# Attention weights of sum scores: one fp32 product max(row, column) in place of two fp8 masks and split fp16 factors

## What is computed

```
h     = relu(layernorm(x));  Wh = h @ W
s, t  = Wh @ a[:128], Wh @ a[128:]
e     = leaky_relu(s[:, None] + t[None, :], 0.2)      # 1024 x 1024 per graph
alpha = softmax(e where adj != 0)                     # rows
x     = x + alpha @ Wh        # 2nd layer; the 4th adds elu(alpha @ Wh)
```

## Time and profile before

| what | value |
|---|---|
| median of 3 runs | 1722.07 us (1720.83 to 1725.84) |
| the profiled execution's own time | 1729.38 us |
| its span | 1727.6 us |
| granted TensorE clock, mean over the span | 0.952 of full speed |
| busy share of the span: PE, DVE, ACT | 87%, 77%, 69% |

### The profile page before, as it was taken

How to read it: one execution, slowest core, us unless ns; L and a number is a source line. 1 busy time by engine, 2 the same in 40 slices (tenths; PEclk the granted TensorE clock), 3 DMA queues, 4 the chain that set the end, 5 groups by cost and what they waited for, 6 DMA issues and landing times. The chain is left out here.

```text
span 1727.6 us, 33849 instructions
## 1 busy us (share of the span) xinstructions
PE 1495.8 (87%) x12740; PEld 1205.6 (70%) x12740; DVE 1323.3 (77%) x3869; ACT 1190.0 (69%) x1841; POOL 182.4 (11%) x201
## 2 busy tenths in 40 slices
PE   3999996999456799999999999999999999999863
PEld 3999996555243676868768687686876868768652
DVE  3666663788356688989889898898998989987753
ACT  2777773222247778889788887888878888785841
POOL 3443320000000100000000000000000000000000
PEclk9999997999777899999999999999999999999976
DMA  9989972566412012222122221222222222111011
GB/s 191 209 197 207 200 159 76 180 242 246 147 49 74 24 57 69 73 62 60 58 80 74 62 58 60 80 74 62 56 62 80 74 62 56 50 56 50 13 30 33
DMA packets 108456, 162.03 MB, mean 94 GB/s; under 512 B 9344, under 2 KB 59136, under 8 KB 106240
## 3 DMA queue, kind: packets, MB, share of 16 engines
q1 hardware_dynamic: 85248, 117.86, 22.8%
q0 software_dynamic: 18432, 33.56, 10.5%
q10 hardware_dynamic: 4608, 8.39, 1.4%
HBM read 151.40 MB, written 41.94 MB: 112 GB/s over the span
## 5 line engine op out<-in xcount | busy, mean ns | idle before, releaser
L1283 PE MATMUL ps<-fac_A,mask_A 128*128 128x258 f16 x2048 | 243.5, 274 | 30.5 <-DVE agg L927 16.7
L1347 PE MATMUL ps<-hV,wts 128*128 128x129 f32 x2048 | 252.6, 279 | 11.4 <-DVE xC L959 4.9
L1283 PE MATMUL ps<-fac_C,mask_C 128*128 128x258 f16 x2048 | 237.7, 274 | 22.1 <-DVE mask_C L922 15.5
L1347 PEld LDWEIGHTS ps<-hV,wts 128*128 128x128 f32 x2048 | 241.2, 194 | 18.4 <-DVE xC L959 12.9
L1283 PEld LDWEIGHTS ps<-fac_A,mask_A 128*128 128x128 fp8e4 x2048 | 196.3, 98 | 72.5 <-DVE agg L927 28.6
L1283 PEld LDWEIGHTS ps<-fac_C,mask_C 128*128 128x128 fp8e4 x2048 | 196.6, 98 | 58.6 <-issue 10.0
L307 ACT ACTIVATE maskT<-ps 128x1024 fp8e4<-128x1024 bf16 x128 | 131.3, 1025 | 54.2 <-PE ps L341 42.2
L1185 ACT ACTIVATE lk<-ps 128x1024 f32<-128x1024 f32 x128 | 131.3, 1026 | 38.8 <-DVE wts L947 23.8
L947 DVE SCALAR_TENSOR_TENSOR wts<-lk,wts 128x1024 f32<-128x1024 f32 x128 | 154.4, 1218 | 2.3 <-ACT wts L1187 2.2
L1335 PE MATMUL ps<-g_hi,ag_hi 128*128 128x512 f16 x256 | 98.9, 386 | 51.4 <-ACT wts L1187 36.0
L1163 ACT ACTIVATE mask_A<-s_row,steep_t_A 128x1024 fp8e4<-128x1024 f32 x128 | 141.3, 1143 | 1.8
(11 more groups left out here) (240 smaller groups left out, 3226.8 us busy)
## 6 DMA issues: line engine op xcount, KB each, us to landing
adj_b<-in_adj POOLq DMA_DIRECT2D x128, 256.0 KB, 9.1
maskT_scratch<-maskT SPq DMA_DIRECT2D x16, 1024.0 KB, 6.8
ring_A<-maskT_scratch SPq DMA_DIRECT2D x64, 256.0 KB, 3.1
off<-maskT_scratch SPq DMA_DIRECT2D x32, 512.0 KB, 4.4
ring_C<-maskT_scratch SPq DMA_DIRECT2D x64, 256.0 KB, 3.6
xa<-in_x SPq DMA_DIRECT2D x16, 512.0 KB, 4.2
whT_scratch<-whT_s ACTq DMA_DIRECT2D x32, 256.0 KB, 6.5
whT_b<-whT_scratch SPq DMA_DIRECT2D x16, 512.0 KB, 4.7
```

The lines of the kernel that those rows point to most:

```text
L1283: last = nc.tensor.matmul(Q_SLOTS[c % 2][:, k, 0:XW], m_fp8[x][:, k, j, c * P:c * P + P], fac[x][:, k, j, :], start=(j == 0), stop=(j == T ...
L1347: last = nc.tensor.matmul(Q_SLOTS[c // 2 % 2][:, c % 2, 0:PW], wts[:, j, c * P:c * P + P], hV[b % 2][:, j, :], start=(j == 0), stop=(j == ...
```

## The change

The weights of A and C are made as an fp32 tile: adjacency byte x max(row_e, least), where `row_e` = exp(0.8 (t + top)) runs along the row and `least` = exp(-0.8 (s - top)) is one value per partition; the remaining factor exp(s - top) goes with the node values (`hP`). Both attentions then use the `weigh` of B (64 fp32 products of 129 columns).

- Gone: `indicate`, `make_below`, `make_above`, `high`, `low`, `up`, `gather`, `quotients`, `attend`, the second set of factors, and the tiles mask_A, mask_C, fac, prod, up_part, agg, s_row, lk.
- New on VectorE: `weights` (one 128 x 1024 product per tile, 16 per round), `shares` (reciprocals of two output tiles' row sums, straight from PSUM), `add` (residuals, half a graph each), `lowest` (a maximum for the check).
- New on ScalarE: `row_power` (exp in place of the copy of the row), `factors` for A, `scaled` (output tile x reciprocal, 24 per round), `relu_hT` for C too. VectorE keeps `factors` for C.
- B: ScalarE copies each score tile once (`keep_scores`), VectorE takes the leaky maximum in place (`leaky`), ScalarE exponentiates from SBUF (`score_exps`). A score slot of PSUM is free after the copy.
- The order of each engine's work in a round is written anew, the order of the loads with it; three fp32 weight tiles of 32 KB per partition replace masks and factors.

The core of the diff:

```diff
+                    def weights(x, b, j):
+                        if j % 2 == 0:
+                            dve.wait_ge(S[x, "ring"][j // 2 % 2], (b * (PAIRS // 2) + j // 4 + 1) * 16)
+                        if j == 0:
+                            dve.wait_ge(S[x, "exp"], b + 1)
+                            dve.wait_ge(S[x, "s_row"], 2 * b + 2)
+                        nc.vector.scalar_tensor_tensor(wts[x][:, j, :], row_e[x][:, :], least[x][:, j:j + 1], ring[x][:, j % MR, :],
+                                                       ALU.max, ALU.mult).then_inc(S[x, "wts"], 1)
+                    def leaky(b, j):
+                        dve.wait_ge(S["B", "kept"], b * T + j + 1)
+                        nc.vector.scalar_tensor_tensor(wts["B"][:, j, :], wts["B"][:, j, :], SLOPE, wts["B"][:, j, :], ALU.mult,
+                                                       ALU.max).then_inc(S["B", "lrelu"], 1)
+                    def shares(x, b, m):
+                        dve.wait_ge(S[x, "tile"], b * T + 2 * m + 2)
+                        r = rec[x][:, 2 * m:2 * m + 2]
+                        nc.vector.tensor_scalar(r.unsqueeze(2), Q_SLOTS[m % 2][:, :, P:PW], TINY, None, ALU.max)
+                        dve.drain()
+                        nc.vector.reciprocal(r, r).then_inc(S[x, "rec"], 1)
+                    def add(x, b, h, new, old):
+                        ts = slice(h * T // 2, (h + 1) * T // 2)
+                        dve.wait_ge(S[x, "quo"], b * PARTS + (h + 1) * PARTS // 2)
+                        nc.vector.tensor_tensor(new[:, ts, :], new[:, ts, :], old[:, ts, :], ALU.add).then_inc(S[x, "done"], 1)
...
+                    def row_power(x, b, h):
+                        nc.scalar.activation(row_e[x][:, h * HALF:(h + 1) * HALF], LAST[x], ACT.Exp, scale=1.0 - SLOPE) \
+                            .then_inc(S[x, "s_row"], 1)
+                    def factors(x, b, h):
+                        for t in range(h * T // 2, (h + 1) * T // 2):
+                            last = nc.scalar.mul(hP[x][:, t, 0:P], VALUES[x][:, t // 3, t % 3, 0:P], hP[x][:, t, P:PW])
+                    def keep_scores(b, j):
+                        nc.scalar.copy(wts["B"][:, j, :], P_SLOTS[j % 2]).then_inc(S["B", "kept"], 1)
+                    def score_exps(b, j):
+                        act.wait_ge(S["B", "lrelu"], b * T + j + 1)
+                        nc.scalar.activation(wts["B"][:, j, :], wts["B"][:, j, :], ACT.Exp, bias=shiftB[:, 0:1]).then_inc(S["B", "exps"], 1)
+                    def scaled(x, b, m):
+                        act.wait_ge(S[x, "rec"], b * PARTS + m + 1)
+                        for c in (2 * m, 2 * m + 1):
+                            last = nc.scalar.mul(new[:, c, :], Q_SLOTS[m % 2][:, c % 2, 0:P], rec[x][:, c:c + 1])
+                        last.then_inc(S[x, "quo"], 1)
...
-                    def attend(x, b, c):
-                        for k in range(2):
-                            for j in range(T):
-                                last = nc.tensor.matmul(Q_SLOTS[c % 2][:, k, 0:XW], m_fp8[x][:, k, j, c * P:c * P + P],
-                                                        fac[x][:, k, j, :], start=(j == 0), stop=(j == T - 1))
+                    def weigh(x, b, c):
+                        if c % 2 == 0:
+                            take(free_q, c // 2 % 2, S[x, "quo"], b * PARTS + c // 2 + 1)
+                        for j in range(T):
+                            if c == 0:
+                                pe.wait_ge(S[x, "exps" if x == "B" else "wts"], b * T + j + 1)
+                            last = nc.tensor.matmul(Q_SLOTS[c // 2 % 2][:, c % 2, 0:PW], wts[x][:, j, c * P:c * P + P], src[:, j, :],
+                                                    start=(j == 0), stop=(j == T - 1))
```

More of the change, by code:

```diff
@@ L746, in gnn_stack_kernel @@
                 for n in ("var", "rstd", "shift", "h", "hT_made", "hT", "s_made", "s_row", "peak", "top_made", "top",
-                          "cols", "steep", "args", "exp", "ind", "wh_made", "prod", "hi", "fac", "below", "mask", "tile", "up", "agg",
-                          "done"):
+                          "us", "te", "exp", "wh_made", "prod", "wts", "tile", "rec", "quo", "done"):
                     S[x, n] = csem(f"{x}_{n}")
@@ L1044, in run @@
[L1044 to L1054 removed]
+                            factors("C", i - 2)
@@ new lines, in run @@
+                        if post:
+                            dve.drain()
+                            dve.wait_ge(S["C", "quo_exp"], i - 2)
+                            nc.vector.scalar_tensor_tensor(old[:, :, :], elu[:, :, :], 1.0, old[:, :, :], ALU.min,
+                                                           ALU.add).then_inc(S["C", "done"], 1)
+                        if GW:
+                            leaky(i - 1, 5)
+                            leaky(i - 1, 6)
+                            leaky(i - 1, 7)
@@ new lines, in run @@
+                        if AA:
+                            shares("A", i, 0)
+                        if nextA:
+                            stats("A", newA, 1)
+                            moments("A")
+                        if AA:
+                            shares("A", i, 1)
+                        if CA:
+                            weights("C", i - 2, 0)
+                        if AA:
+                            add("A", i, 0, newB, oldB)
+                        if nextA:
+                            shifts("A", i + 1)
@@ new lines, in run @@
+                            weights("A", i + 1, 0)
+                            lowest("A")
+                            weights("A", i + 1, 1)
+                        if GW:
+                            shares("B", i - 1, 3)
+                        if nextA:
+                            weights("A", i + 1, 2)
+                        if GW:
+                            highest_share("B", 1)
+                            add("B", i - 1, 1, newC, oldC)
+                            dve.drain()
+                            stats("C", newC, 0)
@@ L1114, in _ @@
+                        if nextA:
+                            weights("A", i + 1, 4)
+                        if CA:
+                            shares("C", i - 2, 2)
+                        if AA:
+                            complement(i, 0)
+                            complement(i, 1)
+                        if nextA:
+                            weights("A", i + 1, 5)
+                            weights("A", i + 1, 6)
                     for k in range(2):
@@ new lines, in run @@
+                        if CA:
+                            row_power("C", i - 2, 0)
+                        if GW:
+                            keep_scores(i - 1, 6)
+                            score_exps(i - 1, 2)
+                            keep_scores(i - 1, 7)
+                        if CA:
+                            row_power("C", i - 2, 1)
+                        if GW:
+                            for j in (3, 4, 5, 6):
+                                score_exps(i - 1, j)
+                        if AA:
+                            scaled("A", i, 0)
```

549 lines of the change are left out of this document (216 added, 333 removed).

## The result

The changed kernel takes **1608.16 us** (median of 4 runs, 1606.74 to 1609.73) against 1723.69 us for the kernel before, run on the same chip (4 runs, 1720.83 to 1725.84): ratio 0.933, 95% interval 0.9313 to 0.9347. Forecast were 1629 us and a range of 1612 to 1668. The profiled execution took 1606.74 us (span 1604.9).

The account below looks back on a forecast made before the run. TensorE's work was taken to bound the rounds. Gains of 71 us in 14 rounds, 6.5 at the start and 15 at the end, together 93, gave 1636, less the 7.3 us offset 1629 us; range 1612 to 1668.

Parts of the forecast that it names:

- What bounds the kernel: Full rounds before: TensorE has work for 67.0 of 71.9 us and stands still for about 4.9.
- Rival 5: A and C: slow fp32 weight loads show after all, 10.3 us more per attention, about 1920 us; chance 0.02.
- length of a full round: Steady rounds: 67.0 us busy, less 0.16 for each of some ten waits, plus 1.3 for overlooked waits: 66.8 us.
- 14 rounds gained: Score start of round 2 to that of round 16: 14 x (71.9 - 66.8) = 71 us gained.
- start, to the scores of round 2: Third phase's beginning: 8.9 us earlier at 533.57, 6.5 at 597.55, since the complement now stands behind A4.
- end, from the scores of round 16: C of the last graph 35 us for 45.4, 3.8 for 6.9 after it, 1.5 in round 16: 15 us gained.
- offset of the profiled execution, kept off: Whole run: the profiled execution's 7.3 us above the median of the runs, left off the forecast time.
- plus about 1.3 for waits I overlook: Each full round: an allowance of about 1.3 us added to TensorE's work for waits not listed.
- VectorE and ScalarE: Busy time per full round: VectorE from 64.1 to 55 us, ScalarE from 59.7 to 44.7 us.
- Which waits go: TensorE's waits for score slots (2.5 us a round) and in A's stretch (1.7 us) go; B keeps one below 0.6.
- Rival 2: VectorE's queue: new in-order waits eat half the gain, 2.5 us per round, 1664 up to 1700 us; chance 0.21.
- Rival 3: New in-order waits eat the whole gain, 5 to 6.5 us per round, 1717 to 1727 us; chance 0.04.

Follow-up runs that it names:

- experiments 1 and 2: Kernel before with only B's part of the change: 1761.0 us (1.0209); the same with exponentials moved behind the later tiles' copies: 1717.57 us (0.9959).
- experiments 5 and 6: Changed kernel with B's mask as a VectorE product, all eight tiles: 1608.57 us; changed kernel with eight extra VectorE maxima a round: 1668.67 us.

## Why the prediction fell short

**What bounds the kernel.** Right. TensorE's standstill was what could be gained, and all of it was. One reading was off: the window of the earlier trace rows is 71.5 us wide, 0.5 short of a round. A full round of the kernel before is

```profile
957.86:1029.83 71.97, 67.47 (x533) 54.22 (x530) 64.58 (x175) 60.16 (x89) 5.38 (x3) 1.00 0.24 67
```

so TensorE had 67.5 us of work, not 67.0, and stood still for 4.5, not 4.9. Of the 6.2 us from there to a round of 65.73, 4.5 are this standstill and 1.7 are shown busy time, for which the forecast had 1.6 (ends of products ahead of waits). TensorE's own work did not grow: the fp32 weight loads, 191 ns against 97, stay hidden. The group from 700 to 1400 us answers to the earlier trace rows:

```profile
L1329 PEld LDWEIGHTS ps<-hP_C,wts_C 128*128 128x128 f32 x1397 | 157.7, 191 | 0.0
```

Rival 5 is out, although PEld is busy through all of three stretches above. The shown loads overlap each other: 128 of 191 ns would be 24.4 us, and A's stretch is 15.17 with its transposes; the group's busy time is 157.7/1397 = 113 ns a load. By the Trainium skill, "TensorE: Matmul & The Clock Gate" (Weight-path perf modes), fp32 weights get no fast load; the 191 ns agree, and the unchanged 112 ns say that it didn't matter here.

**The sum, term by term.**

| term | forecast | measured |
|---|---|---|
| length of a full round | 66.8 | 65.73 |
| 14 rounds gained | 71 | 88.7 |
| start, to the scores of round 2 | 6.5 | 11.2 |
| end, from the scores of round 16 | 15 | 16.9 |
| sum | 93 | 116.8 |
| offset of the profiled execution, kept off | 7.3 | 5.7 before the phase |

**The step that failed is the round of 66.8 us**, and in it "plus about 1.3 for waits I overlook". The work alone was put at 67.0 less 1.6, 65.4 us; with the full round's 67.5 it is 65.9, and 65.73 was measured, all of it work. The 1.3 came from no row, and the trace has no such wait. Most of it would have stood in B's stretch: 66.8 less 17.6 and twice 15.3 leaves 18.6 us there, and it took 17.94, 1.64 us less than before for the 0.4 that I had counted: waits for VectorE's reading of B's output tiles, such as the 0.50 at 1086.77 in the earlier trace rows, went as well. The 12 steady rounds took 65.75 us on average, so they are 12.6 us of the miss.

**Rounds that are not full.** All fourteen were taken as full. The last of them lacks A's preparation and took 61.62 us, 5.2 below the forecast; round 2, at a granted clock of 0.97, took 67.5. The trace of before had this already: its last round was 69.46 us for 71.9. 12.6 and 5.2, less 0.7 for the first, are 17.1 of the 17.7 us that the rounds gave beyond the forecast; the rest is the rounding of 71.9 and 71.

**Start and end.** The first tile was done 11.3 us earlier, 5.7 of them from the earlier phases; the other 5.6 stand for the forecast 6.2. TensorE then waited for the complement in both gaps, as forecast, 6.46 and 8.24 us:

```profile
519.75 0.59 PE L1313 MATMUL ps<-g_hi,ag_hi 128*128 128x512 f16 x1 [6.46 <-DVE off L894]
...
580.67 0.58 PE L1313 MATMUL ps<-g_hi,ag_hi 128*128 128x512 f16 x1 [8.24 <-DVE off L894]
```

But I had let round 1 grow by 2.4 us for it. It shrank by 3.1. Its score stretch fell from 18.40 to 15.33 us: about half of that is waits for the slot, the other half is the granted clock, for behind the gap ahead of it some 14 of its products ran at the lower level's pace (0.43 us apart for 0.22) before and 7 after. That half is luck: in the second profile of the changed kernel it was 13, and from the start of the phase to the scores of round 2 it took 134.4 us in place of 133.07. A's stretch gave 0.8 more, and the two gaps inside the round took 0.9 back. At the end C of the last graph took 33.9 us for the forecast 35; its products came 1.2 us apart, with one late ring (1.25) for the forecast two, as the waits in TensorE's timeline show:

```profile
1565.67 0.80 PE L1329 MATMUL ps<-hP_C,wts_C 128*128 128x129 f32 x2 [0.40 <-DVE wts_C L884]
1567.72 0.80 PE L1329 MATMUL ps<-hP_C,wts_C 128*128 128x129 f32 x2 [1.25 <-DVE wts_C L884]
...
1571.31 14.35 PE L1329 MATMUL ps<-hP_C,wts_C 128*128 128x129 f32 x114 [0.40 <-DVE wts_C L884]
```

**VectorE and ScalarE.** 53.1 us for 55, 43.4 for 44.7. The product was 1.27 us for the 1.21 that I took, for its pointer:

```profile
L884 DVE SCALAR_TENSOR_TENSOR wts_A<-row_A,least_A,ring_A 128x1024 f32<-128x1024 f32 x86 | 108.6, 1274 | 0.0
```

Two in a row stand in 2.47 us, so 1.20 each where one follows another, and the small operations of a pair of shares take about 0.3 us, not 0.48. The largest part of the 2 us is what was taken away: I had priced the residuals' 16 tiles at two operations of 1024 elements, 2.4 us, and the 12 rounds of the earlier trace rows show them as

```profile
L959 DVE SCALAR_TENSOR_TENSOR xC<-ps,recB,xB 128x128 f32<-128x128 f32 x96 | 29.2, 346 | 4.3 <-issue 0.9
L1049 DVE SCALAR_TENSOR_TENSOR xB<-quo,rec,xA 128x128 f32<-128x128 f32 x96 | 26.2, 347 | 0.2 <-issue 0.2
```

which is (29.2 + 26.2)/12 = 4.6 us a round: sixteen small operations cost more than two large ones over the same elements. For `scaled`:

```profile
L1141 ACT ACTIVATE quo<-ps,rec_C 128x128 f32<-128x128 f32 x88 | 27.5, 363 | 63.0 <-DVE rec_C L903 63.0
```

363 ns each, for my 0.41, and two in a row stand in 0.62 us, so the second adds 0.26. From "ScalarE: Activation LUTs" (What ACT_TABLE_LOAD costs) of the Trainium skill comes an estimate of 293 ns with its overlap; the 0.26 us is below it and nearer to it than to my bound, and neither moved the time.

**Which waits go.** Right as a list, wrong as independent terms. The slot wait, the `gather` wait and VectorE's load were priced one by one; experiments 1 and 2 show that B's part alone is worth -36 or +7 us by its order, against the 35 (14 x 2.5) that the sum gave it. They held in sum, with all parts in.

**Rival 2, new in-order waits.** It did not come to pass, but its mechanism is real and near: the complement is ready 1.4 us before TensorE wants it (1041.2 for 1042.58), and experiments 5 and 6 show what 7 to 8 us more on VectorE cost, some 3.4 us a round. The 0.21 for it was not out of place.

**The range.** Its low end, 1612, was to stand for rounds of 65.8 us with start and end at their forecast values; by the sum that is 1629 - 14 x 1.0 = 1615, and 1612 asks for 65.6. The round came out at 65.73, and what else was off on the same side had no room: the short last round 4.2, the start 4.7, the end 1.9, less 1.7 for the longer round 2, some 9 us.

**Slips in the working.** The first tile's terms add up to 486.3, not 486.8. The last graph's, as listed, with 3 us for the two late rings, add up to 38, not 35; 33.9 was measured. Rival 3's 5 to 6.5 us a round give 1699 to 1720, not 1717 to 1727. The first two would have moved the forecast by 0.5 us down and 3 us up, so the 35 was nearer than its own terms by luck.

## What to carry to other kernels

Once the trace names the engine whose work bounds the steady part, forecast that work and list by name any wait you add to it; an allowance for waits that no row shows belongs in the range, not in the central value, and rounds at the edges of a pipeline are to be counted by their own work. A wait's worth isn't a property of the wait: it depends on what stands ahead of the releasing instruction in its in-order queue, and on which engine is next to be late. When the bound engine is full, move a part of its work, no more, to where another one has a gap in that stretch, and leave that one some air (here 12% of the round was enough, with the work placed in gaps, and 7% was not, with the work spread).

## What the runs showed that I had not expected

- An engine need not be full to set the pace. VectorE's 61.4 us against TensorE's 65.7 (93%) lengthened each round by 3.4 us, its 59.8 against some 62.5 (96%) by 3.5; its 56.3 against 64.1 (88%), placed in the gaps, left TensorE without a wait.
- A per-partition pointer in a VectorE product over 1024 fp32 elements costs 0.06 us (1.214 to 1.273); a byte operand in place of an fp32 one costs nothing (1.214 against 1.221 for the fp32 product with a constant).
- fp32 weight loads of 191 ns run fully under pairs of 129-column fp32 records at 112 ns each, with PEld busy 15.1 of 15.1 us and no loss; the shown 191 ns overlap each other, and a load's share of the busy time is 113 ns.
